# Lengths of keys and values as two chains on VectorE, GpSimd's scaling of values five slots on

## The chip, the cores and the metric

The kernel runs on one core of one Trainium2 chip. The metric is the device time of one execution in microseconds; lower is better. The engines of the core are TensorE (PE, with its weight loads PEld), VectorE (DVE), ScalarE (ACT), GpSimd (POOL) and SyncE (SP), which issues the DMAs.

## The reference

Four blocks with a layer norm before each, on x of 4 x 2048 x 256: softmax attention "A" (16 heads of 16), a channel-mixing feed-forward, attention "B", the feed-forward again.

```python
x = x + attn_a(layernorm(x), q_proj, k_proj, v_proj, o_proj)      # causal, 16 heads of 16
x = x + ffn(layernorm(x), W_r, W_k, W_v, mu_r, mu_k)
x = x + attn_b(layernorm(x), W_k, W_v, W_c, beta, key_scale, v_coef, val_scale)
x = x + ffn(layernorm(x), W_r, W_k, W_v, mu_r, mu_k)
```

The change lies in attention B, where keys and values are divided by their lengths, head by head:

```python
k = einsum('hij,bhjd->bhid', coef, k)                  # decayed sum of keys along time
k = k / (norm(k, axis=-1) + 1e-10)
k = k * exp(minimum(10 * key_scale, KEY_SCALE_MAX))
v = (1 - v_coef) * v_shift + v_coef * v
v = v / (norm(v, axis=-1) + 1e-10)
v = v * exp(10 * val_scale)
```

## The kernel before, in words

The work is cut into **slots**. A slot is one group of attention scores (two banks of PSUM, 1024 columns), its exponential on ScalarE and its product with the values. One head group (4 heads of one batch in one attention) takes NG = 68 slots; it works through four query chunks of 512, which end at slots 4, 17, 38 and 67. There are 8 attentions (ATT) of 4 head groups, 32 in all, 2176 slots. TensorE runs three groups of scores ahead of the products.

Beside the slots run **jobs**, one for a chunk of 512 positions of a batch: P (projections of attention A), MB (output projection of B and feed-forward), and MA (output projection of A, feed-forward, and then keys and values of B). A job has a start slot t0 and a table of offsets (T_M, T_B for MA). Each engine goes through the same list of slots in a generator, `interleaved`: at a slot first its part of the attention (`main`), then each job's piece that is due there. The offsets thus set the order of instructions on every engine's own queue; the engines meet by semaphores alone. There are 16 MA jobs, one in each of the four head groups of four attentions (jobs c = 0 to 3), and their t0 is the head group's start minus 4: offset 68 of one job is offset 0 of the next one, in the last of a row that of an MB job.

I call offsets 58 to 80 of an MA job its **tail**. What stands there on the queues:

- VectorE: `u` (57) mixes shifted values; `len` (63) sums the squares of keys (L1386, from buf_a) and of values (L1389, from buf_k), 1024 wide each, into two halves of nw_v (64 + 64 columns), and turns both into 1/length with 15 dependent small operations, 128 columns wide, each waiting for the one before (`settle`): clamp (L1392), `rsqrt` (L1171 to L1180), L1395, L1397, reciprocal (L1399). Then v_fac for GpSimd (L1401) and the keys' factor (L1406). `keys` (69) multiplies k_blk by the factor (L1413, 1024 wide).
- GpSimd: squares of values (L703) at offsets 60 and 62, once ScalarE has copied the transposed values; `vb` (70) writes the values times v_fac into v_st (L709, 1024 wide; L713 after it where c = 0); and the causal masks (L731), one for each diagonal group of the slots.
- The next job's first pieces, at its offsets 0, 2 and 3: `o0` and `o1`, two halves of the output projection on TensorE (32 matmuls each, in one and the same bank of PSUM), which VectorE adds to x (L1315) with statistics behind (L1186); then `ln`, the layer norm's small operations and xn (L1198), which TensorE transposes at `t0` (L884).

At a head group's end VectorE has two further duties. At slot 65 (`maxima`, between o0 and o1) it loads a flag and branches over the code for row maxima when no head of the group needs them; four of the 32 groups need them. At slots 67, 4, 17 and 38 it takes a query chunk's result out of PSUM (L1493, `take`). TensorE's side parts use the bank 7 - seg % 2, the products the other one; the first product of a chunk therefore waits until the side parts in its bank have been emptied, and a side part waits for `take` of the chunk that had its bank.

Of the kernel before, what the change touches and what calls it, by code (L numbers as in the profile page):

```python
# [9 lines left out]
ALU = mybir.AluOpType  # L10
AX_X = mybir.AxisListType.X

P = 128
# [92 lines left out]
class Job:  # L106
# [4 lines left out]
    def __init__(self, kind, b, c, att, t0, off=None):  # L111
# [12 lines left out]
T_M = {"load": -10, "o0": 0, "o1": 2, "ln": 3, "t0": 12, "t1": 14, "diff": 13, "shift": 16, "k0": 18, "k1": 20, "r0": 26,  # L124
       "r1": 28, "f0": 30, "f1": 32, "out": 34}
T_B = {"lnb": 32, "bt0": 40, "bt1": 46, "bk0": 48, "bk1": 50, "bv0": 52, "bv1": 54, "w": 55, "u": 57, "vt0": 59, "vt1": 61,
       "len": 63, "keys": 69, "split": 91, "vb": 70, "low": 94, "store": 98}
T_END = {"load": -10, "o0": 0, "o1": 2, "ln": 2, "t0": 9, "t1": 11, "diff": 10, "shift": 13, "k0": 16, "k1": 18, "r0": 20,
         "r1": 22, "f0": 25, "f1": 27, "out": 30}
PE_PARTS = {"P": ("t0", "t1", "u0", "u1", "u2", "u3", "v0", "v1", "n", "flag"),  # L130
# [125 lines left out]
def hybrid_kernel(nc, t, out):  # L256
    with ExitStack() as ctx:
# [901 lines left out]
        def _(dve):  # L1159
# [6 lines left out]
            def settle():  # L1166
                dve.wait_ge(s_dve, steps[0])

            def rsqrt(n):
                v, y, w = nw_v[:, 0:n], nw_y[:, 0:n], nw_u[:, 0:n]  # L1170
                step(nc.vector.tensor_scalar(y.bitcast(I32), v.bitcast(I32), 1, None, ALU.arith_shift_right))  # L1171
                settle()
                step(nc.vector.tensor_scalar(y.bitcast(I32), y.bitcast(I32), -1.0, float(RSQRT_MAGIC), ALU.mult, ALU.add))
                settle()
                for _ in range(3):
                    step(nc.vector.tensor_tensor(w, y, y, ALU.mult))  # L1176
                    settle()
                    step(nc.vector.scalar_tensor_tensor(w, w, -0.5, v, ALU.mult, ALU.mult))  # L1178
                    settle()
                    step(nc.vector.scalar_tensor_tensor(y, w, 1.5, y, ALU.add, ALU.mult))  # L1180
                    settle()

            def statistics(j, first, end):
                x = x_buf[:, j.at["job"] % 2]
# [3 lines left out]
            def normalize(j):  # L1188
                x = x_buf[:, j.at["job"] % 2]
                settle()  # L1190
                for tb in range(TB):
                    step(nc.vector.bn_aggr(ln_mv[:, tb, :], ln_st[:, tb, :]))
                settle()
                step(nc.vector.tensor_scalar(nw_v[:, 0:TB], ln_mv[:, :, 1], EPS, None, ALU.add))
                settle()
                rsqrt(TB)
                for tb in range(TB):
                    last = nc.vector.tensor_scalar(xn[:, tb, :], x[:, tb, :], ln_mv[:, tb, 0:1], nw_y[:, tb:tb + 1],  # L1198
                                                   ALU.subtract, ALU.mult)
                last.then_inc(s_ln, 1)  # L1200
# [102 lines left out]
            def m_job(j):  # L1303
# [76 lines left out]
                    nc.vector.tensor_copy(vT[:, :, 0:1], vT[:, :, CH:CH + 1]).then_inc(s_vlast, 1)  # L1380
                else:
                    nc.vector.memset(vT[:, :, 0:1], 0.0).then_inc(s_vlast, 1)
                yield j.t0 + j.off["len"]
                nh = TB * H
                dve.wait_ge(s_ksq, 2 * (j.at["ma"] + 1))
                step(nc.vector.tensor_reduce(nw_v[:, 0:nh], buf_a[:, :, :].rearrange("p k (g e) -> p (k g) e", e=DK), AX_X,  # L1386
                                             ALU.add))
                dve.wait_ge(s_vsq, 2 * (j.at["ma"] + 1))
                step(nc.vector.tensor_reduce(nw_v[:, nh:2 * nh], buf_k[:, :, :].rearrange("p k (g e) -> p (k g) e", e=DK),  # L1389
                                             AX_X, ALU.add))  # L1390
                settle()
                step(nc.vector.tensor_scalar(nw_v[:, :], nw_v[:, :], 1.0e-30, None, ALU.max))  # L1392
                settle()
                rsqrt(P)
                step(nc.vector.tensor_tensor(nw_u[:, :], nw_v[:, :], nw_y[:, :], ALU.mult))  # L1395
                settle()
                step(nc.vector.tensor_scalar(nw_u[:, :], nw_u[:, :], NORM_EPS, None, ALU.add))  # L1397
                settle()
                step(nc.vector.reciprocal(nw_y[:, :], nw_u[:, :]))  # L1399
                settle()  # L1400
                nc.vector.tensor_tensor(v_fac[:, :].rearrange("p (t h) -> p t h", t=TB),  # L1401
                                        nw_y[:, nh:2 * nh].rearrange("p (t h) -> p t h", t=TB),
                                        v_scale[:, :].unsqueeze(1).to_broadcast([P, TB, H]),
                                        ALU.mult).then_inc(s_vfac, 1)
# [9 lines left out]
                settle()  # L1414
                yield j.t0 + j.off["split"]
                for m in range(KT):
                    step(nc.vector.transpose(kT[:, m, :], k_blk[:, m, :]))
# [128 lines left out]
```

## Time and profile before

| | us |
|---|---|
| median of 3 runs | 3010.7 (3007.73 to 3011.09) |
| the profiled execution | 3010.78 |
| its span in the trace | 3009.1 |
| TensorE busy | 2862.4 (95%) |
| ScalarE busy | 2232.7 (74%) |
| VectorE busy | 1472.8 (49%) |
| GpSimd busy | 817.1 (27%) |
| mean granted TensorE clock | 0.976 |

The table gives busy time over the whole span. An engine that is busy half of the time can still make another wait at a particular slot, and it is there that the rows further down look. The difference between the profiled execution's time and its span, 1.7 us, lies outside the recorded instructions.

### The profile page before, as it was taken

The numbers are of one execution on the slowest core, as the hardware profiler recorded it, in microseconds if no ns is written. First come the engines' busy times: TensorE is split into PE (matmuls) and PEld (weight loads), VectorE is DVE, ScalarE is ACT, GpSimd is POOL, SyncE is SP. The second block draws the span as 40 slices with busy tenths as digits, with TensorE's granted clock in tenths as the row PEclk, the third lists the DMA queues.
The fourth block names the chain that finished last, engine by engine and source line by source line (L and its number), as shares of the span: only waits on it lengthen the run. The fifth ranks groups of instructions, "written<-read, shape, count | busy, mean of one in ns | idle before, by whom it ended". The sixth has DMA issues, their size and how long they took to land.

```text
span 3009.1 us, 99722 instructions
## 1 busy us (share of the span) xinstructions
PE 2862.4 (95%) x42984; PEld 1302.0 (43%) x42984; DVE 1472.8 (49%) x3579; ACT 2232.7 (74%) x2487; POOL 817.1 (27%) x1246
## 2 busy tenths in 40 slices
PE   6999999999999899998999999999999989999897
PEld 3444444444444344444444444444444434444343
DVE  5322346565556654445344434555665656523544
ACT  2799978787787478784788878778787856788472
POOL 4222223332323222221222222232333322322111
PEclk9999999999999899998999999999999999999898
DMA  5322312222222123222322223222222221222111
GB/s 136 106 83 81 95 53 78 70 73 67 81 71 60 52 67 103 81 76 67 95 81 74 82 89 94 64 78 68 63 75 71 73 66 52 72 72 85 41 62 41
DMA packets 229828, 225.34 MB, mean 75 GB/s; under 512 B 33221, under 2 KB 212933, under 8 KB 229320
## 3 DMA queue, kind: packets, MB, share of 16 engines
q1 hardware_dynamic: 228504, 217.47, 25.3%
q8 instruction: 356, 5.83, 0.8%
q14 instruction: 152, 1.25, 0.1%
q10 hardware_dynamic: 816, 0.79, 0.1%
HBM read 146.80 MB, written 71.32 MB: 72 GB/s over the span
## 4 chain that ended last, share of the span: by engine, by line
PE 72%; DVE 16%; issue 6%; ACT 4%; POOL 1%; SPq 0%; DVEq 0%; DMA 0%; ACTq 0%
PE ps L872 46%; PE ps L1103 23%; ACT probs L828 4%; DVE pmax L1434 3%; PE ps L884 3%; DVE xn L1198 2%; DVE nw_y L1180 1%; DVE nw_u L1178 1%; DVE ln_st L1186 1%; DVE nw_u L1176 1%; DVE x_buf L1315 1%; DVE o_blk L1493 1%; DVE k_blk L1413 1%; DVE nw_v L1389 1%; POOL buf_k L703 0%
## 5 line engine op out<-in xcount | busy, mean ns | idle before, releaser
L828 ACT ACTIVATE probs<-ps 128x1024 f32<-128x1024 f32 x2176 | 2083.1, 1059 | 477.7 <-PE ps L872 474.5
L872 PE MATMUL ps<-q_st,k_st 99*32 99x512 bf16 (+3 forms) x20480 | 1237.4, 349 | 5.0 <-issue 2.4
L1103 PE MATMUL ps<-probs,v_st 128*17 128x512 f32 (+3 forms) x10240 | 1160.7, 532 | 22.4 <-POOL probs L731 13.1
L872 PEld LDWEIGHTS ps<-q_st,k_st 99*32 99x32 bf16 x20480 | 567.0, 96 | 775.7 <-issue 449.6
L731 POOL TENSOR_SCALAR_AFFINE_SELECT probs<-probs 128x256 f32<-128x256 f32 (+1 forms) x896 | 433.4, 501 | 1138.7 <-ACT probs L828 1120.1
L1103 PEld LDWEIGHTS ps<-probs,v_st 128*17 128x17 f32 x10240 | 291.9, 98 | 272.2 <-issue 59.1
L872 PE MATMUL ps<-xT,wT 128*32 128x512 f32 x2048 | 242.6, 594 | 0.0
L1493 DVE STREAM_TRANSPOSE o_blk<-ps 128x512 f32<-128x512 f32 x128 | 91.0, 711 | 269.2 <-PE ps L1103 268.9
L657 POOL TENSOR_TENSOR parts<-rest,parts 128x512 bf16<-128x512 f32 x96 | 120.9, 1260 | 316.7 <-DVE parts L1221 316.7
L1348 DVE SCALAR_TENSOR_TENSOR buf_v<-buf_v,ps 128x512 f32<-128x512 f32 x64 | 44.0, 687 | 272.9 <-PE ps L872 272.9
L1315 DVE TENSOR_TENSOR x_buf<-x_buf,ps 128x512 f32<-128x512 f32 x64 | 43.8, 684 | 217.6 <-PE ps L872 207.2
L872 PE MATMUL ps<-wT,o_in 128*32 128x256 f32 x2048 | 124.3, 380 | 14.5 <-issue 14.5
L872 PE MATMUL ps<-buf_k,wT 128*32 128x512 f32 x1024 | 124.7, 609 | 8.2 <-DVE buf_k L1335 8.0
L872 PEld LDWEIGHTS ps<-xT,wT 128*32 128x32 f32 x2048 | 65.1, 109 | 139.8 <-issue 136.1
L872 PE MATMUL ps<-wT,buf_u 128*32 128x256 f32 x2048 | 121.9, 379 | 1.6 <-issue 1.6
L872 PE MATMUL ps<-wT,buf_a 128*32 128x256 f32 x2048 | 121.6, 379 | 0.6 <-issue 0.5
L884 PE MATMUL ps<-ident,xn 128*128 128x128 f32 x512 | 85.8, 293 | 34.7 <-DVE xn L1198 24.5
L792 ACT ACTIVATE buf_u<-ps 128x512 f32<-128x512 f32 x64 | 38.2, 597 | 99.9 <-PE ps L872 99.9
L884 PEld LDWEIGHTS ps<-ident,xn 128*128 128x128 f32 x512 | 55.8, 145 | 125.1 <-DVE xn L1198 63.1
L1216 DVE TENSOR_TENSOR rest<-ps,parts 128x512 f32<-128x512 f32 x64 | 44.1, 690 | 133.5 <-ACT parts L778 133.5
L681 POOL TENSOR_TENSOR buf_a<-xf 128x512 f32<-128x512 f32 x32 | 33.2, 1037 | 270.3 <-DVE xf L1204 255.5
L1198 DVE TENSOR_SCALAR xn<-x_buf,ln_mv,nw_y 128x256 f32<-128x256 f32 x256 | 99.3, 450 | 2.3
(140 smaller groups left out, 2148.9 us busy)
## 6 DMA issues: line engine op xcount, KB each, us to landing
part_a<-parts SPq DMA_DIRECT2D x192, 128.0 KB
x_buf<-in_L_attn_a_X SPq DMA_DIRECT2D x32, 512.0 KB, 4.6
q_st<-part_a SPq DMA_DIRECT2D x128, 128.0 KB
o_chan<-o_out SPq DMA_DIRECT2D x64, 256.0 KB, 2.4
o_in<-o_chan SPq DMA_DIRECT2D x64, 256.0 KB, 4.6
q_st<-part_b SPq DMA_DIRECT2D x128, 128.0 KB
k_st<-part_a SPq DMA_DIRECT2D x64, 192.0 KB, 2.9
part_b<-parts SPq DMA_DIRECT2D x96, 128.0 KB
```

The lines of the kernel that those rows point to most:

```text
L657: pool.tensor_tensor(parts[:, u % NPARTS, 2, :], rest[:, u % 2, :], parts[:, u % NPARTS, 1, :], ALU.subtract).then_inc(s_low, 1)
L731: last = pool.affine_select(out=o, in_=o, compare_op=ALU.is_ge, fill=0.0, base=0, pattern=[[0, o.shape[1]], [1, P]], channel_multiplier=-1)
L828: nc.scalar.activation(probs[:, g % NP_BUF, :], ps[:, bk:bk + 2, :].rearrange("p a n -> p (a n)"), ACT.Exp, scale=SCALE[ATT[g // (NHG * NG ...
L872: last = pe.matmul(o[c:c + 32], kt[:, c:c + 32], q, **how)
L884: last = pe.transpose(ps[:, part.bank, tb * P:(tb + 1) * P], src[:, tb, kt * P:(kt + 1) * P], ident[:, :])
L1103: last = pe.matmul(ps[32 * j:32 * j + VW, bank, q0:q0 + w], v_st[:, k % 2, kb, hg * HG + j, :], p, start=(kb == 0), stop=(kb >= TB * qc), ...
L1198: last = nc.vector.tensor_scalar(xn[:, tb, :], x[:, tb, :], ln_mv[:, tb, 0:1], nw_y[:, tb:tb + 1], ALU.subtract, ALU.mult)
L1216: nc.vector.tensor_tensor(left, src, high, ALU.subtract).then_inc(s_side[part.bank], 1)
L1315: nc.vector.tensor_tensor(half(x, i), half(x, i), ps[:, part.bank, :], ALU.add).then_inc(s_side[part.bank], 1)
L1348: nc.vector.scalar_tensor_tensor(half(gate, i), half(gate, i), 1.0, ps[:, part.bank, :], ALU.add, ALU.mult).then_inc(s_side[part.bank], 1)
L1434: nc.vector.tensor_reduce(pmax[:, 1 if b0 else 0, qb:qb + 1], src, AX_X, ALU.max).then_inc(s_mx["used"], 1)
L1493: nc.vector.transpose(o_blk[:, sg % 2, :], ps[:, 6 + sg % 2, :]).then_inc(s_o, 1)
```

## The change

The chain `len` becomes two, in a helper `inverse_lengths(sq, at)`, which does the same 16 operations on 64 columns. The keys' chain stands at the new offset `klen` = 58 with the keys' factor and the keys' product right behind it. The values' chain stands at `vlen` = 64 with v_fac behind it. `keys` is gone, and `vb` moves from 70 to 75.

```diff
@@ -124,7 +124,7 @@
 T_M = {"load": -10, "o0": 0, "o1": 2, "ln": 3, "t0": 12, "t1": 14, "diff": 13, "shift": 16, "k0": 18, "k1": 20, "r0": 26,
        "r1": 28, "f0": 30, "f1": 32, "out": 34}
 T_B = {"lnb": 32, "bt0": 40, "bt1": 46, "bk0": 48, "bk1": 50, "bv0": 52, "bv1": 54, "w": 55, "u": 57, "vt0": 59, "vt1": 61,
-       "len": 63, "keys": 69, "split": 91, "vb": 70, "low": 94, "store": 98}
+       "klen": 58, "vlen": 64, "split": 91, "vb": 75, "low": 94, "store": 98}
 T_END = {"load": -10, "o0": 0, "o1": 2, "ln": 2, "t0": 9, "t1": 11, "diff": 10, "shift": 13, "k0": 16, "k1": 18, "r0": 20,
          "r1": 22, "f0": 25, "f1": 27, "out": 30}
 PE_PARTS = {"P": ("t0", "t1", "u0", "u1", "u2", "u3", "v0", "v1", "n", "flag"),
@@ -1166,8 +1166,8 @@
             def settle():
                 dve.wait_ge(s_dve, steps[0])
 
-            def rsqrt(n):
-                v, y, w = nw_v[:, 0:n], nw_y[:, 0:n], nw_u[:, 0:n]
+            def rsqrt(at):
+                v, y, w = nw_v[:, at], nw_y[:, at], nw_u[:, at]
                 step(nc.vector.tensor_scalar(y.bitcast(I32), v.bitcast(I32), 1, None, ALU.arith_shift_right))
                 settle()
                 step(nc.vector.tensor_scalar(y.bitcast(I32), y.bitcast(I32), -1.0, float(RSQRT_MAGIC), ALU.mult, ALU.add))
@@ -1180,6 +1180,19 @@
                     step(nc.vector.scalar_tensor_tensor(y, w, 1.5, y, ALU.add, ALU.mult))
                     settle()
 
+            def inverse_lengths(sq, at):
+                step(nc.vector.tensor_reduce(nw_v[:, at], sq[:, :, :].rearrange("p k (g e) -> p (k g) e", e=DK), AX_X, ALU.add))
+                settle()
+                step(nc.vector.tensor_scalar(nw_v[:, at], nw_v[:, at], 1.0e-30, None, ALU.max))
+                settle()
+                rsqrt(at)
+                step(nc.vector.tensor_tensor(nw_u[:, at], nw_v[:, at], nw_y[:, at], ALU.mult))
+                settle()
+                step(nc.vector.tensor_scalar(nw_u[:, at], nw_u[:, at], NORM_EPS, None, ALU.add))
+                settle()
+                step(nc.vector.reciprocal(nw_y[:, at], nw_u[:, at]))
+                settle()
+
             def statistics(j, first, end):
                 x = x_buf[:, j.at["job"] % 2]
                 for tb in range(first, end):
@@ -1193,7 +1206,7 @@
                 settle()
                 step(nc.vector.tensor_scalar(nw_v[:, 0:TB], ln_mv[:, :, 1], EPS, None, ALU.add))
                 settle()
-                rsqrt(TB)
+                rsqrt(slice(0, TB))
                 for tb in range(TB):
                     last = nc.vector.tensor_scalar(xn[:, tb, :], x[:, tb, :], ln_mv[:, tb, 0:1], nw_y[:, tb:tb + 1],
                                                    ALU.subtract, ALU.mult)
@@ -1380,38 +1393,27 @@
                     nc.vector.tensor_copy(vT[:, :, 0:1], vT[:, :, CH:CH + 1]).then_inc(s_vlast, 1)
                 else:
                     nc.vector.memset(vT[:, :, 0:1], 0.0).then_inc(s_vlast, 1)
-                yield j.t0 + j.off["len"]
+                yield j.t0 + j.off["klen"]
                 nh = TB * H
                 dve.wait_ge(s_ksq, 2 * (j.at["ma"] + 1))
-                step(nc.vector.tensor_reduce(nw_v[:, 0:nh], buf_a[:, :, :].rearrange("p k (g e) -> p (k g) e", e=DK), AX_X,
-                                             ALU.add))
+                of_keys, of_values = slice(0, nh), slice(nh, 2 * nh)
+                inverse_lengths(buf_a, of_keys)
+                fac = nw_v[:, of_keys]
+                step(nc.vector.tensor_tensor(fac.rearrange("p (k b h) -> p k b h", k=KT, h=2),
+                                             nw_y[:, of_keys].rearrange("p (k b h) -> p k b h", k=KT, h=2),
+                                             k_scale[:, :].rearrange("p (k h) -> p k h", h=2).unsqueeze(2)
+                                             .to_broadcast([P, KT, BL, 2]), ALU.mult))
+                settle()
+                keys = k_blk[:, :, :].rearrange("p k (g e) -> p (k g) e", e=DK)
+                step(nc.vector.tensor_tensor(keys, keys, fac.unsqueeze(2).to_broadcast([P, nh, DK]), ALU.mult))
+                settle()
+                yield j.t0 + j.off["vlen"]
                 dve.wait_ge(s_vsq, 2 * (j.at["ma"] + 1))
-                step(nc.vector.tensor_reduce(nw_v[:, nh:2 * nh], buf_k[:, :, :].rearrange("p k (g e) -> p (k g) e", e=DK),
-                                             AX_X, ALU.add))
-                settle()
-                step(nc.vector.tensor_scalar(nw_v[:, :], nw_v[:, :], 1.0e-30, None, ALU.max))
-                settle()
-                rsqrt(P)
-                step(nc.vector.tensor_tensor(nw_u[:, :], nw_v[:, :], nw_y[:, :], ALU.mult))
-                settle()
-                step(nc.vector.tensor_scalar(nw_u[:, :], nw_u[:, :], NORM_EPS, None, ALU.add))
-                settle()
-                step(nc.vector.reciprocal(nw_y[:, :], nw_u[:, :]))
-                settle()
+                inverse_lengths(buf_k, of_values)
                 nc.vector.tensor_tensor(v_fac[:, :].rearrange("p (t h) -> p t h", t=TB),
-                                        nw_y[:, nh:2 * nh].rearrange("p (t h) -> p t h", t=TB),
+                                        nw_y[:, of_values].rearrange("p (t h) -> p t h", t=TB),
                                         v_scale[:, :].unsqueeze(1).to_broadcast([P, TB, H]),
                                         ALU.mult).then_inc(s_vfac, 1)
-                fac = nw_v[:, 0:nh]
-                step(nc.vector.tensor_tensor(fac.rearrange("p (k b h) -> p k b h", k=KT, h=2),
-                                             nw_y[:, 0:nh].rearrange("p (k b h) -> p k b h", k=KT, h=2),
-                                             k_scale[:, :].rearrange("p (k h) -> p k h", h=2).unsqueeze(2)
-                                             .to_broadcast([P, KT, BL, 2]), ALU.mult))
-                yield j.t0 + j.off["keys"]
-                settle()
-                keys = k_blk[:, :, :].rearrange("p k (g e) -> p (k g) e", e=DK)
-                step(nc.vector.tensor_tensor(keys, keys, fac.unsqueeze(2).to_broadcast([P, nh, DK]), ALU.mult))
-                settle()
                 yield j.t0 + j.off["split"]
                 for m in range(KT):
                     step(nc.vector.transpose(kT[:, m, :], k_blk[:, m, :]))
```

VectorE, tail of a job with c = 1, before (nw_v, nw_y, nw_u: the lengths' work columns; k_blk: the keys; x_buf: the next job's x):

```order
L1386 TENSOR_REDUCE nw_v<-buf_a 128x64
L1389 TENSOR_REDUCE nw_v<-buf_k 128x64
L1392 TENSOR_SCALAR nw_v<-nw_v 128x128
...
L1399 RECIPROCAL nw_y<-nw_u 128x128
L1401 TENSOR_TENSOR v_fac<-nw_y,v_scale 128x64
L1406 TENSOR_TENSOR nw_v<-nw_y,k_scale 128x64
L1315 TENSOR_TENSOR x_buf<-x_buf,ps 128x512
L1186 BN_STATS ln_st<-x_buf 128x6 x2
L1468 TENSOR_LOAD flags_a
L1469 COMPARE_AND_BRANCH
```

and in the changed kernel:

```order
L1184 TENSOR_REDUCE nw_v<-buf_a 128x64
L1186 TENSOR_SCALAR nw_v<-nw_v 128x64
...
L1402 TENSOR_TENSOR nw_v<-nw_y,k_scale 128x64
L1408 TENSOR_TENSOR k_blk<-k_blk,nw_v 128x1024
L1184 TENSOR_REDUCE nw_v<-buf_k 128x64
...
L1193 RECIPROCAL nw_y<-nw_u 128x64
L1413 TENSOR_TENSOR v_fac<-nw_y,v_scale 128x64
L1328 TENSOR_TENSOR x_buf<-x_buf,ps 128x512
L1199 BN_STATS ln_st<-x_buf 128x6 x2
L1470 TENSOR_LOAD flags_a
L1471 COMPARE_AND_BRANCH
```

One chain of 15 small operations has become two of 15 on half as many columns, the keys' product stands ahead of the values' sum, and nothing of the lengths is left behind the branch. In all VectorE has 240 operations more, 15 in each of 16 tails.

GpSimd, the same place, before (buf_k: squares of the values; probs: masks):

```order
L703 TENSOR_TENSOR buf_k<-buf_v 128x512 x2
L731 AFFINE_SELECT probs<-probs 128x2x128 x6
L731 AFFINE_SELECT probs<-probs 128x4x128
L731 AFFINE_SELECT probs<-probs 128x2x128
L709 TENSOR_TENSOR v_st<-buf_v,v_fac 128x64x16
L731 AFFINE_SELECT probs<-probs 128x2x128 x5
L731 AFFINE_SELECT probs<-probs 128x4x128
L681 TENSOR_TENSOR buf_a<-xf 128x512
```

and in the changed kernel:

```order
L703 TENSOR_TENSOR buf_k<-buf_v 128x512 x2
L731 AFFINE_SELECT probs<-probs 128x2x128 x6
L731 AFFINE_SELECT probs<-probs 128x4x128
L731 AFFINE_SELECT probs<-probs 128x2x128 x6
L731 AFFINE_SELECT probs<-probs 128x4x128
L709 TENSOR_TENSOR v_st<-buf_v,v_fac 128x64x16
L681 TENSOR_TENSOR buf_a<-xf 128x512
```

The scaling of values, which stood between two masks, now stands behind six more of them, with no mask until the next job's difference (L681). The orders of TensorE, ScalarE and SyncE are the same in both kernels.

## Rows read from the trace of the kernel before

**Rows 1.** The page: busy us, share and count of TensorE; chain by engine; an instruction queue
```profile
PE 2862.4 (95%) x42984; PEld 1302.0 (43%) x42984; DVE 1472.8 (49%) x3579; ACT 2232.7 (74%) x2487; POOL 817.1 (27%) x1246
...
q14 instruction: 152, 1.25, 0.1%
...
PE 72%; DVE 16%; issue 6%; ACT 4%; POOL 1%; SPq 0%; DVEq 0%; DMA 0%; ACTq 0%
```

**Rows 2.** TensorE's waits: waiting line <- releaser: us in all, times, longest
```profile
PE ps L872 <- issue: 19.0, 19, 1.2
PE ps L1103 <- POOL probs L731: 13.1, 9, 2.5
...
PE ps L884 <- DVE o_blk L1493: 10.1, 14, 1.2
...
PE ps L1103 <- DVE x_buf L1315: 3.5, 3, 2.6
```

**Rows 3.** Timeline of TensorE in three tails: start, us, operation, [idle before <- releaser]
```profile
559.40 1.93 PE L872 MATMUL ps<-wT,o_in 128*32 128x256 f32 x32 [1.17 <-issue]
...
565.58 1.05 PE L1103 MATMUL ps<-probs,v_st 128*17 128x512 f32 x8 [2.49 <-POOL probs L731]
...
741.09 1.05 PE L1103 MATMUL ps<-probs,v_st 128*17 128x512 f32 x8 [2.64 <-DVE x_buf L1315]
...
2294.15 1.05 PE L1103 MATMUL ps<-probs,v_st 128*17 128x512 f32 x8 [2.49 <-POOL probs L731]
```

**Rows 4.** Timeline of VectorE in the first of these tails
```profile
550.47 1.22 DVE L1389 TENSOR_REDUCE nw_v<-buf_k 128x64 f32<-128x1024 f32 x1 [4.78 <-POOL buf_k L703]
...
553.00 0.29 DVE L1178 SCALAR_TENSOR_TENSOR nw_u<-nw_u,nw_v 128x128 f32<-128x128 f32 x1
...
554.06 0.47 DVE L1178 SCALAR_TENSOR_TENSOR nw_u<-nw_u,nw_v 128x128 f32<-128x128 f32 x1
...
557.22 0.95 DVE L1399 RECIPROCAL nw_y<-nw_u 128x128 f32<-128x128 f32 x1
558.20 0.37 DVE L1401 TENSOR_TENSOR v_fac<-nw_y,v_scale 128x64 f32<-128x64 f32 x1
558.50 0.21 DVE L1406 TENSOR_TENSOR nw_v<-nw_y,k_scale 128x64 f32<-128x64 f32 x1
558.63 0.67 DVE L1315 TENSOR_TENSOR x_buf<-x_buf,ps 128x512 f32<-128x512 f32 x1
...
563.37 1.38 DVE L1413 TENSOR_TENSOR k_blk<-k_blk,nw_v 128x1024 f32<-128x1024 f32 x1 [3.28 <-issue]
564.79 0.69 DVE L1315 TENSOR_TENSOR x_buf<-x_buf,ps 128x512 f32<-128x512 f32 x1
...
567.12 0.25 DVE L1498 RECIPROCAL rec<-den 128x16 f32<-128x16 f32 x1
...
569.68 0.16 DVE L1178 SCALAR_TENSOR_TENSOR nw_u<-nw_u,nw_v 128x4 f32<-128x4 f32 x1
```

**Rows 5.** Timeline of GpSimd in that tail
```profile
549.40 1.04 POOL L703 TENSOR_TENSOR buf_k<-buf_v 128x512 f32<-128x512 f32 x1 [1.28 <-ACT buf_v L817]
...
553.99 2.47 POOL L731 TENSOR_SCALAR_AFFINE_SELECT probs<-probs 128x256 f32<-128x256 f32 x5 [0.43 <-ACT probs L828]
...
558.65 1.94 POOL L709 TENSOR_TENSOR v_st<-buf_v,v_fac 128x1024 f32<-128x1024 f32 x1 [0.16 <-DVE v_fac L1401]
...
562.91 3.06 POOL L731 TENSOR_SCALAR_AFFINE_SELECT probs<-probs 128x256 f32<-128x256 f32 x5 [1.96 <-ACT probs L828]
```

**Rows 6.** Timeline of VectorE in the first tail of all
```profile
458.32 1.21 DVE L1386 TENSOR_REDUCE nw_v<-buf_a 128x64 f32<-128x1024 f32 x1
464.31 1.22 DVE L1389 TENSOR_REDUCE nw_v<-buf_k 128x64 f32<-128x1024 f32 x1 [4.78 <-POOL buf_k L703]
...
474.65 1.60 DVE L1413 TENSOR_TENSOR k_blk<-k_blk,nw_v 128x1024 f32<-128x1024 f32 x1 [0.72 <-DVE ln_st L1186]
```

**Rows 7.** The keys' product (L1413), whole run: what ended the idle time before it (us, times)
```profile
  issue: 22.1, 7
  DVE ln_st L1186: 5.1, 7
```

More of the change, by code:

```diff
@@ L1382, in m_job @@
                     nc.vector.memset(vT[:, :, 0:1], 0.0).then_inc(s_vlast, 1)
-                yield j.t0 + j.off["len"]
+                yield j.t0 + j.off["klen"]
                 nh = TB * H
                 dve.wait_ge(s_ksq, 2 * (j.at["ma"] + 1))
-                step(nc.vector.tensor_reduce(nw_v[:, 0:nh], buf_a[:, :, :].rearrange("p k (g e) -> p (k g) e", e=DK), AX_X,
-                                             ALU.add))
-                dve.wait_ge(s_vsq, 2 * (j.at["ma"] + 1))
-                step(nc.vector.tensor_reduce(nw_v[:, nh:2 * nh], buf_k[:, :, :].rearrange("p k (g e) -> p (k g) e", e=DK),
-                                             AX_X, ALU.add))
-                settle()
-                step(nc.vector.tensor_scalar(nw_v[:, :], nw_v[:, :], 1.0e-30, None, ALU.max))
-                settle()
-                rsqrt(P)
-                step(nc.vector.tensor_tensor(nw_u[:, :], nw_v[:, :], nw_y[:, :], ALU.mult))
-                settle()
-                step(nc.vector.tensor_scalar(nw_u[:, :], nw_u[:, :], NORM_EPS, None, ALU.add))
-                settle()
-                step(nc.vector.reciprocal(nw_y[:, :], nw_u[:, :]))
-                settle()
-                nc.vector.tensor_tensor(v_fac[:, :].rearrange("p (t h) -> p t h", t=TB),
-                                        nw_y[:, nh:2 * nh].rearrange("p (t h) -> p t h", t=TB),
-                                        v_scale[:, :].unsqueeze(1).to_broadcast([P, TB, H]),
-                                        ALU.mult).then_inc(s_vfac, 1)
-                fac = nw_v[:, 0:nh]
+                of_keys, of_values = slice(0, nh), slice(nh, 2 * nh)
+                inverse_lengths(buf_a, of_keys)
+                fac = nw_v[:, of_keys]
                 step(nc.vector.tensor_tensor(fac.rearrange("p (k b h) -> p k b h", k=KT, h=2),
-                                             nw_y[:, 0:nh].rearrange("p (k b h) -> p k b h", k=KT, h=2),
+                                             nw_y[:, of_keys].rearrange("p (k b h) -> p k b h", k=KT, h=2),
                                              k_scale[:, :].rearrange("p (k h) -> p k h", h=2).unsqueeze(2)
                                              .to_broadcast([P, KT, BL, 2]), ALU.mult))
-                yield j.t0 + j.off["keys"]
                 settle()
@@ L1414, in m_job @@
                 settle()
+                yield j.t0 + j.off["vlen"]
+                dve.wait_ge(s_vsq, 2 * (j.at["ma"] + 1))
+                inverse_lengths(buf_k, of_values)
+                nc.vector.tensor_tensor(v_fac[:, :].rearrange("p (t h) -> p t h", t=TB),
+                                        nw_y[:, of_values].rearrange("p (t h) -> p t h", t=TB),
+                                        v_scale[:, :].unsqueeze(1).to_broadcast([P, TB, H]),
+                                        ALU.mult).then_inc(s_vfac, 1)
                 yield j.t0 + j.off["split"]
```

## The prediction

> **What bounds the kernel now.** I read the page first, then TensorE's waits, then the timelines of the three engines that meet in a tail. TensorE is busy for 95% of the span and holds 72% of the chain that ended last [rows 1]. So nothing that the change does to VectorE or GpSimd counts by itself; only what TensorE stops or starts waiting for does. TensorE works strictly in order, and a gap that closes is time won nearly in full.
>
> In the list of waits [rows 2] three items belong to the tails of MA jobs. The timelines show what they are.
>
> - **The second half waits for the first (o1 for o0).** The 1.17 us before o1 [rows 3] are called "issue", but o0 and o1 use one bank of PSUM, and o1 starts 0.10 us after VectorE's addition (L1315) has emptied it at 559.30 [rows 3, 4]. That addition stood behind the lengths' chain and began at 558.63, right after v_fac and the keys' factor. I count 14 such gaps, 12 of 1.16 or 1.17 us, one of 1.23, one of 0.18; they make up most of the 19.0 us [rows 2].
> - **The long gap at the new head group's first product.** It stands at 565.58, 741.09 and 2294.15 [rows 3] and at four more tails: 2.49, 2.64, 2.20, 0.93, 2.16, 2.13 and 2.49 us, 15.0 us in all. Most of it is put down to GpSimd's mask, yet TensorE starts 0.10 us after the addition for o1, 564.79 + 0.69 [rows 4]; the 2.64 us are put down to that addition. It is late because VectorE stood still for 3.28 us at the branch of slot 65 and then had the keys' product (1.38 us) to do first. The same pause shows before 7 of the 16 keys' products, while seven others wait 0.7 us (5.1 / 7) [rows 7]. The 7 are exactly the tails with the long gap. I call them **slow tails**.
> - **The transposes of t0 wait for `take`** (L884 on L1493), 10.1 us in 14 places [rows 2]; ten of them, 7.5 us, lie in these tails.
>
> Together these gaps are about 38 of the 147 us in which TensorE isn't busy.
>
> **The change part by part.**
>
> *The keys' product leaves the place between branch and addition.* In a slow tail that frees 564.79 - 563.37 = 1.42 us [rows 4], and TensorE's gap shrinks by as much: six of 1.42 and one that is only 0.93 long give 9.4 us. In the other tails the addition for o1 is not late, since o1 itself ends about when the product does; there VectorE is merely ahead by some 1 us afterwards. This assumes that the pause falls on as many tails as before. The trace shows two levels (3.2 and 0.7 us) and nothing in the data that could set them, so the code's position is likely to.
>
> *Two chains instead of one: when does v_fac come?* Let V be the time at which the values' sum starts today, 464.31 or 550.47. The keys' sum starts at V - 5.99 [rows 6], since `len` follows `u` directly, and VectorE idles 4.78 us for GpSimd's squares. The keys' chain goes into that hole. How long is it? Today's 15 operations on 128 columns take 6.5 us from 551.73 to v_fac at 558.20. A two-input operation takes 0.29 us on 128 columns, 0.21 on 64 and 0.16 on 4; beside masks the 128-column one takes 0.47 [rows 4, 5]. Ten of them save 0.07 each; the reciprocal, 0.25 us on 16 columns and 0.95 on 128 [rows 4], is 0.55 on 64 along that line and saves 0.4; four one-input ones save 0.1 together. So a chain of 64 columns takes 6.5 - 1.2 = 5.3 us with as much disturbance by GpSimd as now. Seven operations are stretched by some 0.16 us (0.47 against 0.29); without any of it the chain takes 4.1 to 4.2. Beside the keys' chain run the two squares of values, 2.1 us [rows 5]. No row shows small operations beside such an operation. The bounds are 4.1 (it costs nothing) and 5.3; I take the middle, 4.7, because squares cover 2 us where masks cover 3.7.
>
> Then the keys end at V - 5.99 + 1.25 (sum) + 4.7 + 0.25 (factor) + 1.26 (product) = V + 1.5, between V + 0.9 and V + 2.1. The values' sum could have begun at V; it now starts 1.5 us late. It adds 1.26, its chain 5.1 (masks still run beside it; 4.1 to 5.3), v_fac 0.27: the addition for o0 begins at V + 8.1. Today it begins at 558.63 - 550.47 = V + 8.16. **The shorter chain gives what the late start takes**, and the 1.17 us gap stays: a gain of 0, with ends at V + 6.5 (the whole gap goes, 14 x 1.17 = 16 us won) and V + 8.9 (14 x 0.8 = 11 us lost).
>
> The Trainium skill bears on the unknown here: GPSIMD Engine Reference, section 1, says that the two engines share SBUF interfaces and that VectorE's operations with two SBUF inputs contend. The rows agree for masks (0.29 to 0.47 us). By that rule the squares disturb the keys' chain as masks do, the chain takes 5.0 to 5.3 us, and the addition comes 0.3 to 0.6 us later than in my sum, 4 to 8 us in all.
>
> *GpSimd's scaling moves from between two masks to behind six more.* Its 1.94 us [rows 5] no longer hold up a mask, but no row shows TensorE waiting for that: the gaps named after masks end with the addition. So nothing is won. Its consumers are far off: the gate of the next job at its offset 26, and products of the next attention. Nor is the next job's difference (L681, offset 13) held up. At its new place, though, the scaling runs beside `take` and the layer norm's small operations (0.16 us each, [rows 4]) instead of beside the addition and the statistics. At a third to a half on six or so of them that is 0 to 0.8 us, I take 0.6, on the way to `t0`. In the non-slow tails the lead of 1 us pays for it, and seven waits of `t0` (0.3 to 1.2 us) shrink by 0.4 each, 2.6 us; in slow tails three waits grow by 0.6, 1.8 us. Net 0.8 us won, between -5 and +5.
>
> *Costs that are hidden.* VectorE gets 16 x 4.7 = 75 us more to do, in the hole before the squares arrive. No piece of another engine waits for VectorE in offsets 59 to 63. The keys' product is used by `split` at 91, so its early place costs nobody anything. No order changes on TensorE, ScalarE or SyncE.
>
> **Sum:** 9.4 + 0 + 0.8 = 10.2 us off the profiled execution, 3010.78 - 10.2 = 3000.6, say 3001. The execution lies on the median of the runs (3010.7), so the same number holds against it.
>
> The Trainium skill has a rule on the pause: Runtime: NRT & Kernel Launch, "Instruction fetch mechanics", says that code is fetched in blocks and that a taken branch to a block outside the window stops the engine for a fetch. A queue of the page moved 152 pieces of 1.25 MB / 152 = 8.2 KB [rows 1]. Counting VectorE's instructions in blocks of that size sorts all unflagged branches of before by the one rule "the target lies two blocks on". By that count the 15 added operations move the pauses, from seven tails to six, and the sum would be 11 to 12 us instead of 10.2.
>
> **The rivals.**
>
> - **The gap before o1 closes too.** If the squares leave the small operations alone and the masks disturb 64 columns less, v_fac comes 1 us or more earlier. For it: most durations fall by a quarter. Against it: today's stretched operations. It wins 10 to 16 us more: 2985 to 2991, say 2988.
> - **Hardly anything is left.** The scaling beside the layer norm costs the full 0.8 us in all tails, and v_fac is 0.3 us late: 9.4 - 5 - 4 = 0, about 3008. More long pauses than today would act alike: a pause costs about 1 us of gap even without the product.
> - **Slower: the keys' chain delays the values'.** Mechanism: VectorE is in order, so the values' sum waits for the keys' product although its squares are there. Place: offset 64. Price: every 0.1 us costs 14 x 0.1 = 1.4 us. It decides from an addition at V + 8.9 on (it eats the 10.2 us), and beyond V + 9.3 the kernel is slower by over 0.2%, about 3018. That needs both chains at their upper bounds and more.
> - **The change doesn't do what it says:** the orders show that it does; no weight.
>
> **How the numbers follow.** The forecast (2996 to 3005) gets 0.45, the first rival 0.20, the second 0.26, the third 0.09. The likeliest time is 3001. For 8 in 10 the range takes in the first rival down to 2986 and the second with the near part of the third up to 3014. About 0.2% (6 us) is what a measurement of this kernel can tell from no change. Below 3004.7: 0.45 + 0.20 = 0.65. Within 0.2%: 0.26. Above 3016.7: 0.09.
>
> **What would show it.** In the trace after: the keys' product directly behind the keys' chain, no idle time before the values' sum (now 4.78 us), which starts 0.9 to 2.1 us after the second square; the addition for o0 about 8.1 us after the time V that the squares' end gives; the gap before o1 still about 1.1 us; long gaps at the first product down to about 1.1 us, in six or seven tails; small operations behind `take` above 0.16 us while GpSimd scales. I am wrong if the gap before o1 is gone or has doubled, or if the long gaps don't shrink with the product.

## The result: slower by 18 us, against a forecast of 10 us faster

| | before | changed |
|---|---|---|
| median, us | 3010.52 (3007.73 to 3011.09, 4 runs) | 3028.47 (3027.51 to 3030.82, 4 runs) |
| profiled span | 3009.1 | 3025.8 |
| TensorE busy | 2862.4 | 2858.1 |
| VectorE busy | 1472.8 | 1554.2 |

The ratio is 1.0062, 95% interval 1.0046 to 1.0078. TensorE has the same work; it waits longer. This is the page of the changed kernel, first TensorE's and VectorE's busy time, then the chain by engine (before: [rows 1]):

```profile
PE 2858.1 (94%) x42984; PEld 1290.5 (43%) x42984; DVE 1554.2 (51%) x3819; ACT 2232.0 (74%) x2487; POOL 819.5 (27%) x1246
...
PE 74%; DVE 18%; issue 5%; ACT 2%; POOL 1%; SPq 0%; DMA 0%; DVEq 0%; ACTq 0%
```

TensorE's waits in the changed kernel (line <- releaser: us in all, times, longest), the answer to [rows 2]:

```profile
PE ps L872 <- issue: 29.2, 19, 1.9
PE ps L884 <- DVE o_blk L1495: 27.8, 21, 2.3
...
PE ps L1103 <- POOL probs L731: 5.7, 9, 1.1
...
PE ps L1103 <- DVE x_buf L1328: 2.1, 2, 1.1
```

The gap before o1 has grown from 19.0 to 29.2 us, the wait of t0's transposes for `take` from 10.1 to 27.8 us. The long gaps at a head group's first product have shrunk, 13.1 + 3.5 to 5.7 + 2.1 us. That is 10.2 + 17.7 - 8.8 = 19.1 us more waiting, of 21.0 us by which TensorE's idle time grew in all (146.7 to 167.7 us). Its busy time for the same work is 4.3 us less; the granted clock, treated below, has a part in that.

What VectorE does in the first tail of the changed kernel (start, us, operation), to be read beside [rows 4] and [rows 6]:

```profile
459.13 0.20 DVE L1186 TENSOR_SCALAR nw_v<-nw_v 128x64 f32<-128x64 f32 x1
...
460.35 0.23 DVE L1180 SCALAR_TENSOR_TENSOR nw_y<-nw_u,nw_y 128x64 f32<-128x64 f32 x1
460.61 1.00 DVE L1176 TENSOR_TENSOR nw_u<-nw_y 128x64 f32<-128x64 f32 x1
...
462.94 0.98 DVE L1189 TENSOR_TENSOR nw_u<-nw_v,nw_y 128x64 f32<-128x64 f32 x1
...
464.78 0.23 DVE L1402 TENSOR_TENSOR nw_v<-nw_y,k_scale 128x64 f32<-128x64 f32 x1
465.04 1.23 DVE L1408 TENSOR_TENSOR k_blk<-k_blk,nw_v 128x1024 f32<-128x1024 f32 x1
466.30 1.22 DVE L1184 TENSOR_REDUCE nw_v<-buf_k 128x64 f32<-128x1024 f32 x1
...
472.81 0.67 DVE L1328 TENSOR_TENSOR x_buf<-x_buf,ps 128x512 f32<-128x512 f32 x1
...
479.62 1.88 DVE L1171 TENSOR_SCALAR nw_y<-nw_v 128x4 int32<-128x4 int32 x1
```

GpSimd in the same tail, the two squares and the scaling, in its timeline:

```profile
460.49 1.04 POOL L703 TENSOR_TENSOR buf_k<-buf_v 128x512 f32<-128x512 f32 x1 [3.50 <-ACT buf_v L817]
462.80 1.04 POOL L703 TENSOR_TENSOR buf_k<-buf_v 128x512 f32<-128x512 f32 x1 [1.27 <-ACT buf_v L817]
...
479.53 1.94 POOL L709 TENSOR_TENSOR v_st<-buf_v,v_fac 128x1024 f32<-128x1024 f32 x1
```

Lay the two over each other. The square of 460.49 ends at 461.53; the small operation that began at 460.61 ends at 461.61. The second square ends at 463.84, the operation begun at 462.94 ends at 463.92. The scaling ends at 481.47, the layer norm's operation begun at 479.62 ends at 481.50. Three operations that take 0.17 to 0.23 us alone took 1.00, 0.98 and 1.88 us: each was **held until GpSimd's operation had ended**. It is so in every tail: each of the 32 squares held one operation of the keys' chain, and each of the 16 scalings held one, ten times in the layer norm and six times in `take`. What follows on VectorE's dependent chain moved with them, and TensorE's two waits in that tail grew, from 1.17 to 1.94 us before o1 and from 0.30 to 1.43 us at t0:

```profile
473.58 1.93 PE L872 MATMUL ps<-wT,o_in 128*32 128x256 f32 x32 [1.94 <-issue]
...
485.83 0.63 PE L884 MATMUL ps<-ident,xn 128*128 128x128 f32 x4 [1.43 <-DVE o_blk L1495]
```

Not every operation of VectorE is held. In the kernel before, the scaling at 70 (558.65 to 560.59, [rows 5]) lies over the addition for o0, which reads PSUM, and over the two statistics operations behind it, which read SBUF and take their usual time:

```profile
559.34 0.75 DVE L1186 BATCH_NORM_STATS2 ln_st<-x_buf 128x6 f32<-128x256 f32 x2
```

25 statistics operations lie wholly beside a scaling there, at 0.41 to 0.43 us each; over the whole run they take 0.38 to 0.43 us. In the changed kernel a reciprocal of `take` runs through beside the scaling in its usual 0.25 us in six tails, and the operation behind it is held. So the place at 70 cost next to nothing: only one operation in 16 tails is lengthened there.

### The profile page after: what moved, and what is told of

It is laid out like the page before. It is cut to its first block, busy times and chain, and to the rows that moved or that the text cites. A ratio compares the mean times of both kernels' runs of the same rounds, so it can differ in the third digit from the quotient of the medians.

```text
span 3025.8 us, 99978 instructions
## 1 busy us (share of the span) xinstructions
PE 2858.1 (94%) x42984; PEld 1290.5 (43%) x42984; DVE 1554.2 (51%) x3819; ACT 2232.0 (74%) x2487; POOL 819.5 (27%) x1246
## 3 DMA queue, kind: packets, MB, share of 16 engines
q1 hardware_dynamic: 228504, 217.47, 25.1%
q14 instruction: 154, 1.26, 0.1%
## 4 chain that ended last, share of the span: by engine, by line
PE 74%; DVE 18%; issue 5%; ACT 2%; POOL 1%; SPq 0%; DMA 0%; DVEq 0%; ACTq 0%
PE ps L872 47%; PE ps L1103 23%; DVE pmax L1436 3%; PE ps L884 2%; DVE xn L1211 2%; ACT probs L828 2%; DVE nw_u L1176 1%; DVE ln_st L1199 1%; DVE nw_u L1178 1%; DVE nw_y L1180 1%; DVE o_blk L1495 1%; DVE x_buf L1328 1%; DVE nw_v L1184 1%; DVE nw_y L1171 1%; DVE o_norm L1502 1%
## 5 line engine op out<-in xcount | busy, mean ns | idle before, releaser
L657 POOL TENSOR_TENSOR parts<-rest,parts 128x512 bf16<-128x512 f32 x96 | 121.0, 1260 | 316.8 <-DVE parts L1234 316.8
L884 PE MATMUL ps<-ident,xn 128*128 128x128 f32 x512 | 84.9, 290 | 52.3 <-DVE o_blk L1495 27.8
L872 PEld LDWEIGHTS ps<-wT,o_in 128*32 128x32 f32 x2048 | 70.8, 111 | 76.5 <-issue 46.7
```

What stands on the lines that cost most here:

```text
L657: pool.tensor_tensor(parts[:, u % NPARTS, 2, :], rest[:, u % 2, :], parts[:, u % NPARTS, 1, :], ALU.subtract).then_inc(s_low, 1)
L872: last = pe.matmul(o[c:c + 32], kt[:, c:c + 32], q, **how)
L884: last = pe.transpose(ps[:, part.bank, tb * P:(tb + 1) * P], src[:, tb, kt * P:(kt + 1) * P], ident[:, :])
```

## The experiments

Theory 1 was the hold: a VectorE operation that meets a two-input GpSimd operation waits for its end, so the squares lengthen the keys' chain and the scaling at 75 lengthens `take` or the layer norm. Theory 2: the scaling's new place is harmless, all of the loss is the late start of the values' chain. Theory 3: the late scaling delays somebody who needs its result. All times below are medians; the kernel before ran on the same chips at 3009.2 to 3009.5 us.

### Only the scaling moved

```diff
 (kernel before)
-"vb": 70
+"vb": 75
```

> The kernel before with GpSimd's scaling of values alone moved five slots on (one chain of lengths, keys' product where it was). Theory 1 (an operation of VectorE that meets a GpSimd tensor_tensor is held until that ends): in most tails one of the layer norm's small operations takes 1.6 to 1.9 us beside the scaling instead of 0.17, the transposes of t0 wait 0.9 to 1.5 us longer, and the kernel is 10 to 18 us slower than before. The gap before o1 stays at 1.17 us. Theory 2 (the scaling's place is harmless, and all the loss comes from the values' chain starting late): within 3 us of before.

3028.47 us, ratio 1.0065 (1.0051 to 1.0079): this single number of the change makes all of its loss. The wait of t0's transposes in TensorE's list:

```profile
PE ps L884 <- DVE o_blk L1493: 21.5, 18, 2.0
```

And the operation of the layer norm that is held in the first tail, in VectorE's timeline:

```profile
481.34 1.37 DVE L1194 TENSOR_SCALAR nw_v<-ln_mv 128x4 f32<-128x4 f32 x1
```

Such an operation is held in each of the 16 tails. t0's wait is 21.5 us against 10.1, 11.4 us more, but the kernel lost 19 us by the medians and 16.3 us in the profiled execution. TensorE's busy time grew too, by 8.8 us for the same work (2871.2 against 2862.4), and that leads to the granted clock. Busy time by stretch, with TensorE's granted clock as the last but two number, around the second tail of this kernel:

```profile
560.00:566.00 6.00, 4.71 (x108) 3.03 (x100) 2.96 (x7) 3.12 (x4) 1.12 (x3) 1.00 0.36 89
566.00:572.00 6.00, 4.00 (x32) 1.62 (x36) 5.79 (x9) 3.06 (x4) 4.66 (x6) 0.72 0.00 0
572.00:578.00 6.00, 5.78 (x88) 2.80 (x84) 5.45 (x26) 5.03 (x6) 0.00 (x0) 1.00 0.37 115
```

In the middle stretch TensorE had just stood still for 1.17 and 2.13 us, and the mean clock is 0.72 of 2.4 GHz: more than half of the stretch at 1.2 GHz. Over 15 us behind each of 14 tails (all but the two before groups with row maxima) the mean is 0.89 in 7 tails here, in 3 of the kernel before, in none of the changed kernel. A fall costs about 0.11 x 15 = 1.7 us, so four more of them are 6.6 us, and 11.4 + 6.6 = 18.0 us, a little over the 16.3, since some other waits are shorter. In the changed kernel the three falls fewer would give 5 us back; its busy time is 4.3 us less. Why a fall follows one tail and not another is open (see the last section). Theory 1 stands, theory 2 has fallen.

### The scaling back at 70 in the changed kernel

```diff
 (changed kernel)
-"vb": 75
+"vb": 70
```

> The changed kernel with the scaling of values back at offset 70; the two chains and the early keys' product stay. Theory 1: the layer norm's small operations are 0.16 us again, t0's waits fall from some 23 us in all to under 10, and it gains 10 to 15 us on the changed kernel: 3013 to 3018 us. The gap before o1 stays at 1.94 us. Theory 2: as slow as the changed kernel, 3026 to 3030 us.

3003.17 us, ratio 0.9983 (0.9974 to 0.9992): the rest of the change is a small gain, and the scaling's place costs 25 us in this kernel, twice what I expected. Its waits:

```profile
PE ps L872 <- issue: 27.9, 19, 1.9
...
PE ps L884 <- DVE o_blk L1495: 6.2, 9, 1.1
```

The gap before o1 is nearly what it was (1.85 us a tail, not 1.94); t0's wait fell by 21.6 us.

### The keys' product back behind the branch

```diff
 (kernel with two chains, scaling at 70)
-... keys' product behind the keys' factor, offset 58
+yield j.t0 + j.off["keys"]      # 69
+... keys' product
```

> As the kernel with the scaling back at 70, but the keys' product is done at offset 69 again, behind the branch; the two chains stay at 58 and 64. If the values' sum is late by the keys' chain and product together, the addition for o0 comes 1.26 us earlier and the gap before o1 falls from 1.94 to about 0.7 us (14 tails, 17 us won), while the long gaps at a head group's first product come back from 0.8 to about 2.2 us in some seven tails (10 us lost): 3007 to 3013 us. If the two chains' operations are disturbed by something else and the product's place doesn't matter, the gap before o1 stays at 1.9 us: 3023 us or more.

3006.57 us, ratio 0.9991 (0.9982 to 1.0000). The second tail on TensorE, o1 and the head group's first product:

```profile
557.30 1.93 PE L872 MATMUL ps<-wT,o_in 128*32 128x256 f32 x32 [1.03 <-issue]
...
563.11 1.05 PE L1103 MATMUL ps<-probs,v_st 128*17 128x512 f32 x8 [2.13 <-POOL probs L731]
```

The gap before o1 falls from 1.85 to 1.03 us, the long gap returns (0.7 to 1.1 us with the product ahead, 2.13 here). The product's place is an exchange: 0.8 us in every tail against 1.2 us in half of them. The product's 1.26 us don't show in full before o1, because the values' chain now meets GpSimd's masks at other operations. Its sum starts 1.26 us earlier after the second square (1.2 us behind it, not 2.5), but from the start of the sum to the addition it takes 6.86 us (549.66 to 556.52 in this tail) against 6.41 us with the product ahead (552.57 to 558.98). That leaves the 0.8 us.

### Values first, the keys' chain in the next job's hole

```diff
 (changed kernel)
-"klen": 58, "vlen": 64, "vb": 75
+"klen": 58, "vlen": 63, "kinv": 85, "keys": 91, "vb": 70
 yield klen: sum of the keys' squares into a tile of its own (k_sum)
 yield vlen: sum of the values' squares, their chain, v_fac
+yield kinv: the keys' chain from k_sum, the keys' factor
+yield keys: the keys' product
```

> Values first: the keys' squares are summed at offset 58 into a tile of their own, the values' chain of 64 columns stands at 63 with nothing of the keys before it, the keys' chain goes to offset 85 (the hole before the next take), its product to 91, the scaling of values to 70. If the late start of the values' chain is what costs, its addition for o0 comes about 6.5 us after the second square instead of 8.9, the gap before o1 is gone (1.17 us in before, 1.94 in the changed kernel), the long gaps are about 0.6 us, and the kernel takes 2978 to 2988 us, faster than both. If 64 columns gain nothing because GpSimd's masks set the pace, the gap before o1 stays near 1.1 us: 2995 to 3003 us.

2974.57 us, ratio 0.9886 (0.9871 to 0.9901): faster than both, and slightly below the range I gave. Two of TensorE's waits:

```profile
PE ps L873 <- issue: 5.1, 6, 1.5
PE ps L885 <- DVE o_blk L1500: 4.9, 8, 0.8
```

VectorE's timeline in the first tail, with the values' sum, v_fac and the addition for o0:

```profile
463.43 1.22 DVE L1402 TENSOR_REDUCE nw_v<-buf_k 128x64 f32<-128x1024 f32 x1 [4.78 <-POOL buf_k L704]
...
469.59 0.23 DVE L1405 TENSOR_TENSOR v_fac<-nw_y,v_scale 128x64 f32<-128x64 f32 x1
469.74 0.68 DVE L1327 TENSOR_TENSOR x_buf<-x_buf,ps 128x512 f32<-128x512 f32 x1
```

The addition begins 6.3 us after the values' sum, not 8.2 as in the kernel before, and the gap before o1 is gone (the item had 29.2 us in the changed kernel and 19.0 us before). The same halves of the chain that cost in the changed kernel gain here, where nothing of the keys' chain but its sum and no held operation stands in front of the values' chain. The run changes several things together, and its 35 us are not divided among them: the waits at the first product and at t0 are shorter too, and no fall of the clock stands behind its tails.

### The same, with the scaling at 75

```diff
 (kernel with values first)
-"vb": 70
+"vb": 75
```

> The kernel with values first and the keys' chain at 85, with the scaling moved from 70 to 75 alone. Theory 1: it loses 12 to 22 us by the held operation, to 2987 to 2997 us. If the loss needs a late VectorE (which this kernel hasn't got, its lead over TensorE being some 2 us longer), it stays within 4 us of 2974.6 us.

3003.91 us, ratio 0.9976 (0.9967 to 0.9985): 29 us lost by the scaling's place alone, more than I had written. VectorE's lead didn't protect it:

```profile
PE ps L885 <- DVE o_blk L1500: 27.4, 21, 2.0
```

That is 22.5 us more than the 4.9 us above, from one held operation in each tail. TensorE's busy time is 7.2 us more, with four falls of the clock behind tails where the other kernel has none. The place has three prices, 19, 25 and 29 us, in part because the scaling meets other operations: summed over the 16 tails, and each against the shortest of its line, the held ones are lengthened by 17.7 us in the kernel before, by 23.8 us in the changed one and by 25.1 us here.

### The squares on ScalarE

```diff
 (changed kernel)
-pool.tensor_tensor(buf_k[:, i, :], half, half, ALU.mult)
+nc.scalar.activation(buf_k[:, i, :], ps[:, part.bank, :], ACT.Square)
```

> The changed kernel with the squares of values made by ScalarE straight from PSUM (one more activation before each of its two copies) and not by GpSimd. Theory 1 (an operation of VectorE beside a GpSimd tensor_tensor is held until it ends): the two operations of about 1.0 us in each keys' chain are gone, the keys' chain takes 4.1 us instead of 5.7, the addition for o0 comes 1.5 us earlier and the gap before o1 falls from 1.94 to about 0.4 us; the scaling's hold in the layer norm stays: 3004 to 3012 us. Theory 2 (the keys' chain is slow by itself): the gap stays at 1.9 us and ScalarE's extra work adds to it: 3028 us or more.

3011.26 us, ratio 1.0005 (0.9996 to 1.0014), 17 us less than the changed kernel. The keys' chain in the second tail, its first operation and its factor:

```profile
546.54 0.20 DVE L1182 TENSOR_SCALAR nw_v<-nw_v 128x64 f32<-128x64 f32 x1
...
550.64 0.23 DVE L1398 TENSOR_TENSOR nw_v<-nw_y,k_scale 128x64 f32<-128x64 f32 x1
```

4.10 us from the one to the other, 5.65 in the changed kernel (459.13 to 464.78). The two holds were 1.55 us of it. The gap before o1 is gone altogether, where I had expected 0.4 us to stay; in exchange TensorE waits 0.30 us for an exponential in each tail.

### Values first and the squares on ScalarE

```diff
 (kernel with values first, scaling at 70)
-pool.tensor_tensor(buf_k[:, i, :], half, half, ALU.mult)
+nc.scalar.activation(buf_k[:, i, :], ps[:, part.bank, :], ACT.Square)
```

> Values first, keys' chain at 85, scaling at 70, and the squares of values made by ScalarE. The values' chain can start about 0.6 us earlier and nothing else waits for the squares; TensorE's gap before o1 is gone already. If ScalarE has room: 2970 to 2976 us; if its two further activations a tail push the exponentials back: 2976 to 2990 us.

It took 2984.96 us, ratio 0.9920 (0.9906 to 0.9933): 10 us more than with GpSimd's squares. With the gap before o1 gone there is nothing to win. TensorE waits for an exponential in each of the 16 tails, 4.6 us in all, and its idle time grows by 5.0 us. Its busy time grows by 7.2 us as well, which these runs don't explain.

### One more operation on GpSimd, which nobody waits for

```diff
 (kernel before; scaling at 70)
+yield j.t0 + 75
+step(pool.tensor_tensor(idle[:, :], idle[:, :], idle[:, :], ALU.mult))   # 128 x 1024, bf16
```

> The kernel before, with one more GpSimd tensor_tensor of 1024 bf16 columns at offset 75, on a tile of its own that nobody else reads or writes; everything else, the scaling at 70 too, stays. Theory 1 (VectorE is held by what GpSimd does at that place): an operation of VectorE between take and xn is held for up to the length of the added one, t0's waits grow by 10 us or more in all, and the kernel takes 3018 to 3030 us. Theory 3 (the moved scaling delayed somebody who waits for its result): no hold, within 3 us of before.

The added tile is bf16 because a float32 one doesn't fit into SBUF beside the others; the float32 version has no time.

3025.12 us, ratio 1.0052 (1.0038 to 1.0065): 15.6 us for an operation without a consumer, so theory 3 has fallen too. VectorE's timeline in one tail:

```profile
568.31 0.70 DVE L1498 STREAM_TRANSPOSE o_blk<-ps 128x512 f32<-128x512 f32 x1
569.04 1.31 DVE L1501 TENSOR_SCALAR den<-o_blk 128x16 f32<-128x16 f32 x1
570.38 0.25 DVE L1503 RECIPROCAL rec<-den 128x16 f32<-128x16 f32 x1
```

GpSimd's timeline there:

```profile
568.42 1.89 POOL L718 TENSOR_TENSOR idle<-idle 128x1024 bf16<-128x1024 bf16 x1
```

The added operation ends at 570.31, the held one at 570.35. The transpose that reads PSUM runs through untouched beside it, in its usual 0.70 us.

With one input instead of two:

```diff
-step(pool.tensor_tensor(idle[:, :], idle[:, :], idle[:, :], ALU.mult))
+step(pool.tensor_scalar(idle[:, :], idle[:, :], 1.0, None, ALU.mult))
```

> As the last, but the added GpSimd operation is a tensor_scalar with one input. Theory 1 as read from the masks (one input too, and a hold of 0.1 to 0.3 us each): a short hold, and 3009 to 3016 us. If any GpSimd operation holds VectorE for its whole length, and this one is as long as the two-input one: as slow as that.

3013.69 us, ratio 1.0014 (1.0005 to 1.0023): 4 us, not 16. The GpSimd operation is even longer, but it holds VectorE over its first part alone. GpSimd's timeline in one tail:

```profile
566.72 2.77 POOL L718 TENSOR_SCALAR idle<-idle 128x1024 bf16<-128x1024 bf16 x1
```

VectorE's timeline there:

```profile
567.32 0.45 DVE L1501 TENSOR_SCALAR den<-o_blk 128x16 f32<-128x16 f32 x1
567.81 0.25 DVE L1503 RECIPROCAL rec<-den 128x16 f32<-128x16 f32 x1
568.10 0.42 DVE L1505 TENSOR_TENSOR o_norm<-o_blk,rec 128x256 f32<-128x256 f32 x1
```

The first operation takes 0.45 us where the two-input GpSimd operation made the same line take 1.31. It ends 1.05 us after GpSimd's start and 1.72 us before its end, and the next ones take their usual time. So it is in 12 of the 16 tails, in two of them with 0.98 us for 0.17; in three a second operation is held at GpSimd's end, by 0.4 us. Summed over the 16 tails VectorE's operations are lengthened by 5.6 us, against 17.0 us beside the two-input one. The length of GpSimd's operation alone doesn't set the price. Whether the second input does or the kind of operation (tensor_scalar against tensor_tensor), these two runs don't separate.

The scaling in two halves:

```diff
 (kernel before)
-"vb": 70, one tensor_tensor of 4 x 256 columns
+"vb": 75, two of 2 x 256 columns
```

> The kernel before with the scaling at 75 and cut into two operations of 512 columns. If a hold lasts to the end of the GpSimd operation that is under way: two operations of VectorE are held, for some 0.8 us each, with others running freely between, and the time is that of the uncut one, 3024 to 3030 us. If the hold is a fixed cost of one clash, two clashes cost more: over 3035 us; if short operations are let by, under 3018 us.

3026.38 us, ratio 1.0053 (1.0040 to 1.0067), the same as uncut. VectorE's timeline in one tail:

```profile
570.89 0.47 DVE L1500 TENSOR_SCALAR den<-o_blk 128x16 f32<-128x16 f32 x1
571.39 0.25 DVE L1502 RECIPROCAL rec<-den 128x16 f32<-128x16 f32 x1
571.68 0.95 DVE L1504 TENSOR_TENSOR o_norm<-o_blk,rec 128x256 f32<-128x256 f32 x1
```

GpSimd's timeline there, both halves in one row:

```profile
570.27 2.07 POOL L711 TENSOR_TENSOR v_st<-buf_v,v_fac 128x512 f32<-128x512 f32 x2
```

Two operations are held, one by each half (0.47 for 0.18 and 0.95 for 0.42, the second until 572.63, the halves' end being 572.34), and 0.25 us of work get through between. The sum of the holds is 0.8 us in this tail, where the uncut scaling holds one operation by 1.2 us (a PSUM transpose covers the first part in both). Over the 16 tails it is 15.8 us against 17.7, and t0's waits are 22.1 us against 21.5: the cut saves almost nothing. The profiled execution was the slowest of the five, with eight falls of the clock behind the 14 tails, against seven in the uncut kernel and three in the kernel before.

## Why the prediction was wrong, step by step

- **The keys' product leaves the place behind the branch, 9.4 us: right.** The long gaps were 2.49, 2.64, 2.20, 0.93, 2.16, 2.13, 2.49 us; in the changed kernel seven of 0.66 to 1.00 us, 5.9 in all, 9.1 us less. The exchange test gives the mechanism.
- **The pause at the branch: nearly right.** The prediction's count of blocks of code gave six pauses in tails; there are seven, five of them in other tails than before. The four runs that leave VectorE's program as it was (vb75_alone, extra75b, extra75_copy, halves75) have them in the same seven tails as the kernel before, so the pauses move with VectorE's code. So far the trace agrees with the sentence on Runtime: NRT & Kernel Launch, "Instruction fetch mechanics", in the Trainium skill. No run here shows a fetch or the size of a block, and the gain of 1 to 2 us didn't come.
- **"The shorter chain gives what the late start takes": wrong, and the first step that failed.** Its term was the keys' chain, 4.7 us between bounds of 4.1 and 5.3. It takes 5.65 us, outside the bounds; with the squares on ScalarE it takes 4.10, the lower bound. I sized the disturbance by the masks, as some tenths spread over many operations; it is one operation a square, held for what is left of 1.04 us. The values' chain was right, 5.0 us for 5.1 (467.55 to 472.57). With V = 463.87, just behind the end of the second square, the addition for o0 begins at V + 8.9, the far end of the range, not V + 8.1. The gap is 1.94 us, not 1.17: 10.2 us lost instead of 0.
- **"No row shows small operations beside such an operation": true, and still the miss.** A large one was there to be read in the kernel before. VectorE's timeline has the subtraction L1219 twice:

```profile
589.54 0.69 DVE L1219 TENSOR_TENSOR rest<-kT,parts 128x512 f32<-128x512 f32 x1
...
591.07 1.53 DVE L1219 TENSOR_TENSOR rest<-kT,parts 128x512 f32<-128x512 f32 x1
```

  and GpSimd's timeline the two-input L657:

```profile
590.77 1.28 POOL L657 TENSOR_TENSOR parts<-rest,parts 128x512 bf16<-128x512 f32 x1 [3.77 <-DVE parts L1221]
```

  0.69 us alone, 1.53 beside GpSimd: it starts 0.3 us into the other's 1.28, waits for 592.05 and ends 0.55 us later. Two rows of one line with different durations were the price of the hold.
- **GpSimd's scaling beside the layer norm, 0.8 us won between -5 and +5: wrong, and the larger miss.** The held operation takes 1.88 us for 0.17 in the first tail. t0's waits grew by 17.7 us. The term was mis-sized by the same mistake: 0.6 us a tail, where the 16 holds are 0.6 to 1.7 us, 1.5 on the mean. VectorE's lead of 1 us did not pay for it. By experiment, the place of the scaling costs 19 us in the kernel before, 25 in the changed one, 29 in the best.
- **What speaks for the page.** GPSIMD Engine Reference, section 1, in the Trainium skill says that the two engines share interfaces and contend. I gave it 4 to 8 us outside the sum, by the masks' size. The trace agrees with the rule, but the chain took 5.65 us where I had 5.0 to 5.3 by it. I had taken only VectorE's operations with two inputs from that section; of the ten held in the layer norm all have one.
- **The rival "slower" came true in its first half.** The addition at V + 8.9 is the point that I had named for no change. The other half came from the scaling, for which I had no rival on the slower side, only a share of "hardly anything is left".
- **The clock was in no term.** Three falls of the kernel before, each behind a long gap, are missing in the changed one, 5 us in the change's favour at 1.7 us each. That the shorter gaps did it is not shown.

## What to carry to other kernels

Before a GpSimd operation with two inputs is moved, list what VectorE does at its new place: put it beside operations that read PSUM, beside statistics, or beside idle time, not beside a chain of small dependent operations that a busy engine waits for. Price it at the rest of GpSimd's operation, once for each. And when a chain is split so that a part is ready sooner, start the part that someone waits for first; the other one goes into the next hole, not into the one just before.

## What the runs showed of the hardware that I had not expected

- A two- or one-input arithmetic operation of VectorE on SBUF that meets a two-input GpSimd operation is held until that ends: 1.00 and 0.98 us for 0.23, 1.88 for 0.17, 1.31 for 0.18. One such operation is held for each GpSimd operation, in the same way by two halves. A mask of GpSimd, with one input and 0.41 us long, holds small operations until its end too (552.16 to 552.57 in the kernel before, the operation begun at 552.25 ends at 552.64); a one-input tensor_scalar of 2.77 us held them over its first 1.05 us, and in three of 16 tails at its end, but not between.
- Statistics operations and reciprocals read SBUF and are not held: 0.41 to 0.43 us and 0.25 us beside a two-input GpSimd operation, as elsewhere. Nor is a transpose from PSUM, 0.70 us.
- The granted clock of TensorE fell from 2.4 to 1.2 GHz for 3.4 us behind some tails, at some 1.7 us each. In the kernel before, TensorE had stood still for 1.2 us and again for over 2 us in all three of these tails; but 2.64 us at 741 brought a fall, 2.49 us at 565 none. In the values-first kernel with the scaling at 75, four tails brought one with no gap before o1, 0.9 to 1.5 us at the first product and 1.9 to 2.0 us at t0; the changed kernel, with 1.9 us before o1 and up to 2.3 us at t0, had none. All this is of the 14 tails without row maxima. The runs don't show which gaps decide.
- VectorE's pause at a taken branch has two levels, 0.7 and about 3 us, and moves with VectorE's code: with 15 operations more in each tail five of the seven long ones in tails stand in other head groups.
